# Two token buffers: batches 0 and 1 as one loop of 16 tiles, rows normalized in place

## The reference, cut to what matters

```
x = x + tanh(g_xattn) * xattn(layernorm(x), ctx)      # x: 4 batches, 1024 tokens, 256
x = x + tanh(g_ffn)   * ffn(layernorm(x))

xattn: x1 = LN(m1); x2 = LN(ctx)                      # ctx: 77 rows of 192 for each batch
       q, k, v = x1@Wq+bq, x2@Wk+bk, x2@Wv+bv
       softmax(q k^T / 16) v @ Wo + bo
ffn:   gate = softmax(x@gate_w + gate_b);  top 2 of 8 experts
       sum over the two of gate * (relu(x@w1[e]+b1[e]) @ w2[e] + b2[e])   # hidden 1024
```

## Time and profile before

| | us |
|---|---|
| median of 3 runs | 618.15 (616.84 to 618.96) |
| the profiled execution | 619.11 |
| its span, first to last instruction | 617.4 |
| TensorE busy in the span | 508.6 |
| VectorE, ScalarE, GpSimd busy | 406.3, 417.2, 252.8 |
| first product of the slots (hidden(0)) starts at | 154.62 |
| mean granted TensorE clock | 0.884 of full speed |

### The profile page before, as it was taken

The page is one execution under the profiler, slowest core; times in us unless marked ns, Lnnn a source line. Parts: engine busy times, 40 slices in busy tenths (PEclk is TensorE's granted clock), DMA queues, the critical chain, the costliest instruction groups (busy, mean ns, idle before and its releaser), DMA issues.

```text
span 617.4 us, 15633 instructions
## 1 busy us (share of the span) xinstructions
PE 508.6 (82%) x4717; PEld 426.4 (69%) x4718; DVE 406.3 (66%) x1173; ACT 417.2 (68%) x1061; POOL 252.8 (41%) x270
## 2 busy tenths in 40 slices
PE   6887504540888999878999987899999999999991
PEld 3456303420777888766788876789898988999981
DVE  3238798669785677778667777877655665566660
ACT  1567866435765667656667766678888888888880
POOL 3100226730287322328842232784777433332332
PEclk9575555555999999999999999999999999999996
DMA  6709620940543322443432242343333333233221
GB/s 168 280 3 372 236 71 19 302 162 22 195 113 83 54 36 38 104 105 88 98 69 47 37 104 37 89 116 63 67 69 54 55 56 50 48 53 55 36 28 17
DMA packets 47633, 57.07 MB, mean 92 GB/s; under 512 B 6855, under 2 KB 43197, under 8 KB 47423
## 3 DMA queue, kind: packets, MB, share of 16 engines
q1 hardware_dynamic: 32223, 36.60, 19.6%
q0 software_dynamic: 14064, 18.55, 17.2%
q10 hardware_dynamic: 1264, 0.93, 0.5%
HBM read 33.19 MB, written 24.49 MB: 93 GB/s over the span
## 4 chain that ended last, share of the span: by engine, by line
PE 49%; DVE 17%; ACT 9%; issue 9%; POOL 6%; DMA 4%; SPq 1%; ACTq 1%; DVEq 1%; POOLq 0%
PE hid L1700 8%; PE hid L1704 7%; PE bank L1722 6%; PE bank L1724 6%; PE bank L1723 6%; PE hid L1703 4%; PE hid L1701 4%; ACT pool L845 4%; DVE pool L1384 3%; DVE w1l L948 2%; POOL xs L578 2%; PE bank L1681 2%; DVE w2l L948 2%; DMA pool<-in_L_ffn_w_dram 2%; PE bank L1563 1%
## 5 line engine op out<-in xcount | busy, mean ns | idle before, releaser
L640 POOL DMA_INDIRECT out_dram<-pool,idx x71 | 118.5, 1669 | 217.5 <-DVE pool L1399 166.4
L845 ACT ACTIVATE pool<-hid,b1s 128x128 f32<-128x128 f32 x568 | 167.8, 373 | 10.0 <-PE hid L1704 2.7
L1700 PE MATMUL hid<-pool,w1h 128*128 128x256 f16 x568 | 155.2, 273 | 13.2 <-DVE pool L1384 9.4
L1722 PE MATMUL bank<-w2h,pool 128*128 x568 | 154.8, 272 | 4.3 <-issue 3.7
L1704 PE MATMUL hid<-pool,w1h 128*128 128x256 f16 x568 | 155.2, 273 | 0.0
L1724 PE MATMUL bank<-w2h,pool 128*128 x568 | 154.8, 272 | 0.0
L1723 PE MATMUL bank<-w2l,pool 128*128 x568 | 154.8, 272 | 0.0
L1384 DVE TENSOR_TENSOR pool<-hid,pool 128x512 f32<-128x512 f32 x142 | 96.4, 689 | 71.3 <-ACT pool L845 71.3
L1701 PE MATMUL hid<-pool,w1l 128*128 128x128 f16 x568 | 124.7, 219 | 0.0
L1703 PE MATMUL hid<-pool,w1l 128*128 128x128 f16 x568 | 124.6, 219 | 0.0
L854 ACT ACTIVATE pool<-pool 128x512 f16<-128x512 f32 x142 | 89.8, 636 | 44.1 <-DVE pool L1384 44.0
(11 more groups left out here) (254 smaller groups left out, 713.5 us busy)
## 6 DMA issues: line engine op xcount, KB each, us to landing
pool<-in_L_ffn_w_dram SPq DMA_DIRECT2D x12, 1024.0 KB, 11.3
pool<-xs SPq DMA_DIRECT2D x71, 132.5 KB, 2.2
xb<-in_x_dram SPq DMA_DIRECT2D x4, 1024.0 KB, 6.6
out_dram<-xb SPq DMA_DIRECT2D x4, 1024.0 KB, 4.9
out_dram<-pool,idx POOLq DMA_INDIRECT x71, 3.9
w1h<-in_L_ffn_w_dram SPq DMA_DIRECT2D x1, 1024.0 KB, 5.1
w1l<-in_L_ffn_w_dram SPq DMA_DIRECT2D x1, 1024.0 KB, 7.6
w2h<-in_L_ffn_w_dram SPq DMA_DIRECT2D x1, 1024.0 KB, 9.7
```

The source lines that it names most:

```text
L640: g.indirect_dma_start(out=out_rows, out_offset=bass.IndirectOffsetOnAxis(ap=idx[s % U][:, 0:1], axis=0), in_=y2[s % 3], in_offset=None, c ...
L845: a.activation(hb[:, c * P:(c + 1) * P], bank[c // 2][:, (2 * (c % 2) + 1) * P:2 * (c % 2 + 1) * P], ACT.Identity, bias=b1s[:, ds(e * NH + ...
L1700: t.matmul(o, wh, xhl, start=True, stop=False)
L1722: t.matmul(o, hh[s % 2][:, hs], wh, start=c == 0, stop=False)
```

## The change

xb, st, mv, vv and rs exist twice, for even and odd batches, each load of x has a semaphore of its own buffer, and batch 1's x is loaded early, behind experts 0 and 1. xf is gone: rows are normalized in place in xb, after the store of the batch has landed, and the probabilities have four small tiles pr. For batches 0 and 1 the normalization moves from VectorE to ScalarE (eight activations with scale rs and bias nmr = -mean * rs; for batches 2 and 3 it stays on VectorE). zpad is gone: the zero rows are made in xext. The two loops of 8 tiles become one of 16, and batch 0's routing is written into its second half.

```diff
             load_expert(0)
             load_expert(1)
+            load_x(1)
...
             store_x1(0)
-            next_x(0)
             sp.wait_ge(s_lo, 5)
             load_expert(6)
+            store_x1(1)
             sp.wait_ge(s_lo, 6)
             load_expert(7)
-            store_x1(1)
+            next_x(0)
...
             for s in range(U, S):
                 load_rows(s)
-                if s == AT[2] + 16:
+                if s == U + 1:
+                    next_x(1)
+                if s == AT[2] + 14:
                     store_x1(2)
-                if s == AT[2] + 18:
-                    next_x(2)
-                if s == AT[3] + 16:
+                if s == AT[3] + 14:
                     store_x1(3)
...
@@ GpSimd @@
             root_1(0)
+            root_1(1)
             root(0)
             root(1)
             root_2(0)
+            root(2)
             token_ids(0)
-            root(2)
-
-            root_1(1)
-            scatter_rows(0, 0, KO * T)
+            scatter_rows(0, 0, 10)
             root_2(1)
+            scatter_rows(0, 10, KO * T)
             root(3)
             token_ids(1)
...
@@ ScalarE @@
+            def rows_norm_2(b):
+
+                act.wait_ge(s_nmr, b + 1)
+                act.wait_ge(s_outd, (b + 1) * 16)
+                for i in range(T):
+                    a.activation(xb[b % 2][:, i, 0:D], xb[b % 2][:, i, 0:D], ACT.Identity, bias=nmr[:, i:i + 1],
+                                 scale=rs[b % 2][:, i:i + 1]).then_inc(s_xn, 1)
...
+            for k in range(NB * T + 4):
+                if k < NB * T:
+                    rows_copy(k // T, k % T)
+                if 1 <= k <= NB * T:
+                    softmax_exp((k - 1) // T, (k - 1) % T)
+                if 2 <= k < NB * T + 2:
+                    prob_copy((k - 2) // T, (k - 2) % T)
+                if k in (0, 1):
+                    hi_part(0, k)
+                if k in (2, 3):
+                    hi_part(1, k - 2)
+                if k == 4:
+                    square(2, 0)
+                    square(2, 1)
                 if k in (5, 6):
                     square(3, k - 5)
+                if k == 7:
+                    square(4, 0)
+                    square(4, 1)
                 if k in (8, 9):
-                    square(4, k - 8)
...
+                    square(5, k - 8)
+                if k in (10, 11):
+                    hi_part(2, k - 10)
+                if k in (12, 13):
+                    hi_part(3, k - 12)
+                if k == 15:
+                    gate_exp(0)
+                    hi_part(4, 0)
+                if k == 16:
+                    hi_part(4, 1)
+                    rows_norm_2(0)
+                if k == 17:
+                    high_rows(0, 0, T)
+                    hi_part(5, 0)
+                if k == 18:
+                    hi_part(5, 1)
+            square(6, 0)
+            square(6, 1)
             gate_exp(1)
+            square(7, 0)
+            square(7, 1)
+            rows_norm_2(1)
             for e in (6, 7):
                 hi_part(e, 0)
                 hi_part(e, 1)
...
@@ VectorE @@
+            for k in range(NB * T + 5):
+                tile_of(k)
+                if k in (1, 2):
+                    lo_part(0, k - 1)
+                if k in (3, 4):
+                    lo_part(1, k - 3)
+                if k == 8:
+                    scales_start(1)
                 if k == 9:
...
                     scales(1)
+                if k in (10, 11):
+                    lo_part(2, k - 10)
+                if k == 13:
+                    mean_2(0)
+                    scales_start(2)
+                if k == 14:
+                    choose_1(0)
+                    norm_bias(0)
+                    scales(2)
+                if k == 15:
+                    choose_2(0)
+                    lo_part(3, 0)
+                if k == 16:
+                    gates(0)
+                    lo_part(3, 1)
+                if k == 17:
+                    places(0)
+                    lo_part(4, 0)
+                if k == 18:
+                    low_rows(0, 0, T)
+                    lo_part(4, 1)
+                if k == 19:
+                    lo_part(5, 0)
                     counts_1(0)
+                if k == 20:
+                    lo_part(5, 1)
                     counts_2()
...
+            tables(0)
             mean_2(1)
+            choose_1(1)
+            norm_bias(1)
+            choose_2(1)
+            gates(1)
             scales_start(3)
...
+            places(1)
             scales(3)
...
+            lo_parts(6)
             lo_parts(7)
-            rows_norm_2(1, 0, T)
```

More of the change, by code:

```diff
@@ L272, in gated_attention_and_routed_experts @@
         s_w = sem("s_w")
-        s_x = sem("s_x")
+        s_x = [sem(f"s_xin{k}") for k in range(2)]
         s_b1 = sem("s_b1")
@@ L521, in _ @@
             g = nc.gpsimd
-            g.memset(zpad[:], 0.0).then_inc(s_turn, 1)
+            g.memset(xext[:, 0, :], 0.0).then_inc(s_turn, 1)
             g.memset(ident[:], 0.0).then_inc(s_const, 1)
@@ L543, in _ @@
             pool.wait_ge(s_turn, 1)
-            for j in range(2):
-                g.iota(zpad[:, j, TC:XW].bitcast(I32), [[0, 1]], base=(B - 1) * L + T - 2 + j,
-                       channel_multiplier=T).then_inc(s_tok, 1)
+            g.iota(xext[:, 0, TC:XW].bitcast(I32), [[0, 1]], base=(B - 1) * L + T - 2,
+                   channel_multiplier=T).then_inc(s_tok, 1)
             pool.wait_ge(s_const, 16)
@@ L576, in scatter_rows, with pad_rows @@
                         pool.wait_ge(s_x16l, (b + 1) * T)
-                        pool.wait_ge(s_tok, 2 + b + 1)
+                        pool.wait_ge(s_tok, 1 + b + 1)
                     g.indirect_dma_start(out=xs, out_offset=bass.IndirectOffsetOnAxis(ap=dest[:, n:n + 1], axis=0),
                                          in_=xext[:, i, :], in_offset=None).then_inc(s_scat, 16)
+            def pad_rows():
+                pool.wait_ge(s_scat, B * KO * T * 16)
+                g.memset(xext[:, 0:2, 0:TC], 0.0).then_inc(s_padz, 1)
+                for j in range(2):
+                    g.iota(xext[:, j, TC:XW].bitcast(I32), [[0, 1]], base=(B - 1) * L + T - 2 + j,
+                           channel_multiplier=T).then_inc(s_padz, 1)
             def scatter_pads(n):
@@ L661, in _ @@
                 scatter(s)
+                if s == CNT[3] + 7:
+                    pad_rows()
                 if CNT[3] + 8 <= s < CNT[3] + 8 + E:
@@ L766, in high_rows @@
                     act.wait_ge(s_scat, b * KO * T * 16)
-                a.copy(xe16[:, first:last, 0:D], xf[:, first:last, :]).then_inc(s_x16h, last - first)
+                else:
+                    act.wait_ge(s_zst, 16)
+                a.copy(xe16[:, first:last, 0:D], xb[b % 2][:, first:last, 0:D]).then_inc(s_x16h, last - first)
             def gate_exp(b):
@@ L1267, in _ @@
-            for k in range(T + 5):
-                tile_of(0, k)
-                if k in (1, 3):
-                    lo_part(1, k // 2)
+                if 1 <= k < NB * T + 1:
+                    score_in((k - 1) // T, (k - 1) % T)
+            for k in range(NB * T + 5):
[6 more added lines that the diff above has]
+                    scales_start(1)
@@ L1271, in _ @@
                 if k == 9:
-                    scales_start(1)
-                if k == 10:
                     scales(1)
-            mean_2(0)
-            lo_part(2, 0)
-            choose_1(0)
-            choose_2(0)
-            lo_part(2, 1)
-            gates(0)
-            places(0)
-            rows_norm_2(0, 0, T)
-            lo_part(3, 0)
-            scales_start(2)
-            low_rows(0, 0, T)
-            scales(2)
-            stats_1(1, 0, T)
-            mean_1(1)
-            lo_part(3, 1)
@@ L1299, in _ @@
                     counts_2()
-                if k == 10:
-                    tables(0)
+            tables(0)
             mean_2(1)
+            choose_1(1)
+            norm_bias(1)
+            choose_2(1)
+            gates(1)
             scales_start(3)
-            choose_1(1)
+            places(1)
             scales(3)
-            choose_2(1)
-            lo_part(6, 0)
-            gates(1)
-            places(1)
-            lo_part(6, 1)
+            lo_parts(6)
             lo_parts(7)
-            rows_norm_2(1, 0, T)
@@ L1586, in position @@
                 pe.wait_ge(s_x1, (b + 1) * T)
-                pe.wait_ge(s_nrmc, (2, 4, 4, 4)[b])
+                pe.wait_ge(s_nrmc, 4 if b else 3)
                 if b:
```

203 lines of the change are left out of this document (83 added, 120 removed).

## The result

The changed kernel takes **624.44 us** (median of 5 runs, 621.85 to 624.59) where the kernel before takes 617.38 (5 runs, 616.84 to 618.96): 1.0097 of it, 95% interval 1.0077 to 1.0116. It is slower, by some 6 us by the ratio (the two medians are 7.1 us apart). I had forecast 619.4 with a range that ended at 623.0, so the measured time lies above the range. The profiled execution is the shortest of the five (621.85 us, span 620.1), 2.7 us over the span of the old one.

The account below looks back on a forecast made before the run. VectorE, ScalarE and waits bound the run-up, TensorE the slots; GpSimd's scatters were to decide. Last residue part +2.5 us, less 1.28 behind it, net +1.2: profiled 619.1 becomes 620.3, forecast 619.4 us, range 614.5 to 623.0.

Parts of the forecast that it names:

- the sum of the path through the scatters: Run-up: batch 0's scatters hold gates(1) and the scales, moving the last residue part from 154.1 to 156.6, net +1.2 us.
- the alternation there: Merged loop, steps 10 and 11: VectorE and ScalarE wait on each other, with gaps of about 2.4 us before expert 2's residue parts.
- Both waits are gone: Run-up: the waits for batch 1's variance root (3.67 us) and expert 6's load (10.0 us) vanish after the change.
- Last scatter starts at 140.0: GpSimd: batch 0's scatters start at 115.35 behind low_rows(0); 15 distances of 18.9 + 3.8 and a root of 1.9 us.
- the cover that I called used up at 0.46: ScalarE's eight moved normalizations, taken at 0.36 us each, fit before VectorE needs the rows; even at 0.46 they cost 0.
- My mean of four: GpSimd: four residue parts in the old trace delayed the scatters by 1.27 us each; three now, so 3.8 us.
- rival (a): Full lock-out: each of three residue parts holds GpSimd 2.34 us, adding 3.2; 622.6 us; chance 0.22 with other missed waits.
- 156.6: End of the run-up's last residue part in us, from the scatters' landing at 142.5 through gates(1) and scales; before 154.1.
- Come 1.28 earlier: Behind the last residue part, ScalarE's cast of batch 1's rows and h_bias(0) gain 1.28 us, through to the first h_sum.
- Expert 7: 140.7, 2 us before the scatters: Other path to the same point: expert 7's load, squares and norms end at 140.7, 2 us ahead of the scatters' path.
- my list of moves without a waiter: Later or earlier moves said to cost nothing: store_x1(2), pad_rows in slot 36, the earlier loads of batches 2 and 3.
- Rival (b): The alternation in steps 10 to 12 doesn't occur: 4.9 us go, 614.5 us; chance 0.19 with other shortenings of the loop.

Follow-up runs that it names:

- no_loads: The changed kernel without the loads of experts 6 and 7, their steps working on stale data of experts 4 and 5; 1.0045 of the kernel before.
- store_behind: The changed kernel with the store of batch 1's x1 issued behind the load of expert 7 instead of ahead of it; 1.0061 of the kernel before.
- scales_first: The changed kernel with the scales of experts 6 and 7 ahead of gates(1) and places(1), batch 1's normalization behind their high parts; 1.0045 of the kernel before.
- norm_back: The changed kernel with the row normalizations of batches 0 and 1 back on VectorE, still in place; 1.0108 of the kernel before.
- with two loops: The changed kernel's buffers and early load, but two loops in the old order, normalizations on VectorE; 0.9990 and 0.9966 of the kernel before on two chips.
- fast2: Second buffer with two unmerged loops, plus reordering that fills the waits for experts 6 and 7; 0.9841 and 0.9866 of the kernel before on two chips.
- step_later: The changed kernel with both residue parts of expert 2 one step later, at steps 11 and 12; 1.0009 of the kernel before.
- a_third: The changed kernel unedited on another chip; 658.46 us against 653.23 for the kernel before, ratio 1.0075.
- a_fourth: The changed kernel unedited on another chip; 650.97 us against 647.45 for the kernel before, ratio 1.0040.
- a_again: The changed kernel unedited on another chip; 651.35 us against 648.33 for the kernel before, ratio 1.0053.

## Why the prediction was wrong

**The step that failed is the sum of the path through the scatters.** It put the first y_sum 1.2 us later, and the traces have it 3.8 later (4.3 from the first copy of nrm). Its two largest errors are in the start of the last scatter: the residue parts beside the scatters cost more than priced, and so did the normalizations on ScalarE, priced at 0.

What held: the root of batch 1's first variances is out of the chain; the statistics are hidden; ScalarE at the high part of expert 2 (ended 79.42, forecast 79.55); the alternation there (idle 3.19 and 2.57, forecast 2.4 each); and above all the mechanism, that batch 0's scatters hold gates(1) and gates(1) the scales. no_loads and store_behind show it by experiment, and scales_first that they do so by 1.5 us. "Both waits are gone" held only of the chain: ScalarE's wait for expert 6 grew, from 7.4 to 10.8 us.

The terms of the sum one by one:

- **"Last scatter starts at 140.0": it started at 141.87.** low_rows(0) ended at 115.28 and not 114.45, 0.8 late: 0.3 of it VectorE's wait for the cast, since ScalarE's eight normalizations took 4.03 us, 0.50 each, above my whole interval of 0.30 to 0.46; the cover that I called used up at 0.46 was overrun. The other 0.5 us are 0.1 at the second residue part of expert 2 and 0.4 spread over steps 12 to 18. norm_back shows that the move is right even so. From there the first scatter took 0.2 more to start, and the 15 distances 25.5 instead of 24.6: the root between them cost 1.6 and not 1.9, but the three residue parts cost 1.32, 1.69 and 1.84 us (2.28, 2.65 and 2.80 against 0.96), 4.85 and not 3.8. My mean of four hid what sets the size: **how much of the residue part is left when the scatter starts**. The three residue parts (115.20, 118.39 and 122.79, each 2.3 us long) had 1.2, 1.8 and 2.0 us left at the starts of the scatters. In the trace of the kernel before the scatters that started at 103.34, 105.76, 111.07 and 114.53 found 1.3, 1.6, 1.1 and 1.3 us left and took 1.16, 1.52, 0.93 and 1.21 us more; those that started just ahead of a residue part or within 0.1 us of its start took at most 0.3 more. The Trainium skill (SBUF — State Buffer, section Who interferes with whom) has the exclusive lock held for the whole instruction, and the traces agree with it to 0.15 us once only the rest of the instruction is counted. So the prediction read the rule wrongly, in "not in size" and in rival (a)'s full 2.34 us for each residue part. One such pair of the kernel before, VectorE and then GpSimd:

```profile
105.07 2.34 DVE L948 SCALAR_TENSOR_TENSOR w2l<-pool,scl,w2h 128x2048 f16<-128x2048 f32 x1
```

```profile
105.76 2.48 POOL L578 DMA_INDIRECT xs<-xext,dest  x1 [0.30 <-issue]
```

- **"156.6": it was 158.84.** The start above gives 1.9 of the 2.2; the landing (the gate write came 2.6 after that start, forecast 2.5) and the steps behind it (14.3, forecast 14.1) the rest.
- **"Come 1.28 earlier": 0.9.** The last residue part moved by 4.72 and the first y_sum by 3.81. The gain did reach the first h_sum, which moved by 3.25 (159.75 to 163.00), and not the second, which moved by 3.81 (160.78 to 164.59). VectorE waited for h_bias on ScalarE there, and h_bias for TensorE (0.30 us at 163.27). hidden(0) began at 154.62 before and 159.30 now, and TensorE had the 2.4 GHz level back 2.3 us after it before and 3.5 us after it now. Before and now:

```profile
156.00:157.00 1.00, 1.00 (x9) 0.80 (x8) 0.84 (x5) 0.22 (x1) 0.00 (x0) 0.54 0.86 331
```

```profile
162.00:163.00 1.00, 1.00 (x10) 0.80 (x9) 0.00 (x0) 0.97 (x4) 0.00 (x0) 0.61 1.15 451
```

- **"Expert 7: 140.7, 2 us before the scatters":** its squares ended at 142.7 and norms(3) at 143.6, 0.9 us before the landing. The first square came 13.3 us after the issue (125.56) where I took 10 to 11. The load of batch 2's rows, issued 0.8 us behind it, was on my list of moves without a waiter; that it slowed expert 7 is likely, and not tested. The sum also missed gate_exp(1), which stands ahead of these squares and ended at 138.1, so an earlier load would have gained 0.75 us at most.

Together 2.6 us too few at the first y_sum: +3.8 where I had +1.2, and 622.0 instead of 619.4. The rest to 624.44 (2.4 us) is in no trace. The two profiled executions differ by 2.7 us and the medians by 7.1; the old one is longer than all five of its kernel and the new one the shortest of its five. Over four chips the mean (4.1 us) agrees with the +3.8 to 4.3 of the traces; that the first chip shows 6 to 7 stays open.

The larger fault is one of question. I followed the new order along the path and priced its terms, and never asked **how long VectorE's idle time was in all, and when expert 7's load could be issued**. Both are plain in the order: the weave puts eight tiles of batch 1 (8 x 1.46 = 11.7 us of VectorE) among and ahead of the residue parts of experts 3 to 5, of which those of 4 and 5 free the buffers for experts 6 and 7. Expert 7 is issued at 125.15 woven and its squares start at 138.82; with two loops it is issued at 113.67 and they start at 126.73. Then the tiles are used up, and VectorE idles 6.7 and 4.95 us while loads and scatters run. fast2 does the reverse and gains 9 to 10 us. Rival (b), which I gave 0.19 with the others of its kind, had the right size (4.9; step_later gained 4.3); I priced it as something that might not occur, when it was a loss that the kernel had and one line could remove.

## What to carry to other kernels

Work that doesn't depend on a long transfer is the cover for it: put whatever frees the buffer first, start the transfer, and keep the independent tiles for the time that it takes. A second buffer is worth what its wait cost (3.2 to 3.4 us of the run-up here), and merging the loops around it is a separate decision to be priced by itself. When two engines alternate on a wait, shift one of them by a step before anything else.

## What the runs showed of the hardware

**The return of TensorE's clock shifts the front by 1.1 us.** Windows of a_third and then of a_fourth, the same program on two chips (the last but two column is the granted clock):

```profile
36.00:37.00 1.00, 1.00 (x5) 0.64 (x4) 0.00 (x0) 0.52 (x1) 1.00 (x1) 0.92 0.00 0
```

```profile
36.00:37.00 1.00, 1.00 (x4) 0.65 (x3) 0.12 (x1) 0.32 (x1) 0.80 (x1) 0.50 0.00 0
...
38.00:39.00 1.00, 0.65 (x5) 0.52 (x3) 0.16 (x1) 0.43 (x1) 0.12 (x1) 0.93 0.00 0
```

TensorE was busy in both; in one it got the 2.4 GHz level back just after 36 us, in the other 2 us later. The first copy of nrm came at 37.52 and 38.64, and everything up to the slots is shifted by that. Two traces of one kernel can thus differ by 1.1 us in the run-up without any edit. On the first chip the level came back at 37.5 us in the kernel before (granted clock 0.77 between 37 and 38 us) and at 36.5 in the changed one (0.76 between 36 and 37).

**The first passes through the slots are slow on some chips.** The changed kernel between 170 and 190 us, on the first chip and then in a_again:

```profile
170.00:190.00 20.00, 17.93 (x188) 15.14 (x186) 16.50 (x59) 14.23 (x38) 16.01 (x17) 1.00 0.58 166
```

```profile
170.00:190.00 20.00, 16.36 (x137) 12.10 (x136) 10.99 (x35) 9.59 (x26) 13.33 (x15) 0.83 0.51 145
```

The second y_sum followed the first after 5.8 us on the one and after 12.8 on the other, and the like came again at slots 17 to 20 and 32 to 34; TensorE's waits there are put down to issue. By these stretches a_again falls 27.5 us behind the first chip's profile, about what that chip is slower by with the kernel before (648.33 against 617.38). Their cause wasn't looked into. Only ratios taken on one chip are used above for this reason.
